# Expert tiles of 128 rows instead of 256 in a mixture-of-experts block, up and down projections alternating in halves

## The reference

```python
x = x + tanh(g_xattn) * cross_attention(layernorm(x), ctx, frac, ...)      # 16 x 128 rows of 256
xf = layernorm(x).reshape(2048, 256)
top_w, top_i = top_k(xf @ gate_w + gate_b, 2)                              # 2 of 8 experts per row
combine = sum(softmax(top_w)[:, :, None] * one_hot(top_i, 8), axis=1)
for e in range(8):
    h = gelu(xf @ w1[e] + b1[e])                                           # 256 -> 1024
    out = out + combine[:, e:e + 1] * (h @ w2[e] + b2[e])                  # 1024 -> 256
shared = gelu(xf @ ws1 + bs1) @ ws2 + bs2
x = x + tanh(g_ffn) * (out + shared)
```

## Time and profile before

| | us |
|---|---|
| device time, median of 3 runs | 719.77 |
| lowest and highest of them | 719.32, 729.58 |
| span of the profiled execution, first to last instruction | 702.4 |
| median less the span (the profiled execution has no other time recorded) | 17.4 |

### The profile page before, as it was taken

How to read it: one execution, slowest core, us unless ns; L and a number is a source line. 1 busy time by engine, 2 the same in 40 slices (tenths; PEclk the granted TensorE clock), 3 DMA queues, 4 the chain that set the end, 5 groups by cost and what they waited for, 6 DMA issues and landing times.

```text
span 702.4 us, 16222 instructions
## 1 busy us (share of the span) xinstructions
PE 652.4 (93%) x4755; PEld 557.8 (79%) x4767; DVE 449.9 (64%) x1444; ACT 348.5 (50%) x1026; POOL 327.7 (47%) x291
## 2 busy tenths in 40 slices
PE   4799999999999999996969999999999999999991
PEld 3698888998888888895545656999898998989880
DVE  2987535468789588547796854866575665655640
ACT  2567554376678577534853756433243342433410
POOL 4596525357676666513677743233232332323323
PEclk9679555599899698556898999999999999999996
DMA  8022221022233223101234458332332323323222
GB/s 270 32 66 65 65 64 52 11 65 64 64 89 101 54 72 85 46 31 45 79 125 158 142 174 215 121 61 33 58 46 44 60 35 54 55 34 45 24 24 30
DMA packets 44514, 51.91 MB, mean 74 GB/s; under 512 B 9281, under 2 KB 38593, under 8 KB 44353
## 3 DMA queue, kind: packets, MB, share of 16 engines
q1 hardware_dynamic: 36320, 41.23, 20.9%
q0 software_dynamic: 8160, 10.26, 8.6%
HBM read 32.79 MB, written 18.69 MB: 73 GB/s over the span
## 4 chain that ended last, share of the span: by engine, by line
PE 76%; DVE 10%; issue 4%; ACT 3%; POOL 2%; DMA 1%; SPq 0%; DVEq 0%; ACTq 0%; POOLq 0%
PE bank L1113 69%; PE bank L1173 5%; DVE W L805 3%; ACT W L611 1%; PE bank L1326 1%; DVE hbuf L903 1%; DVE W L775 1%; DMA out<-xres 1%; PE bank L1193 1%; DMA out<-xres,idu 1%; POOL out L547 1%; ACT W L590 0%; DVE xT L910 0%; PE bank L1254 0%; SPq L346 0%
## 5 line engine op out<-in xcount | busy, mean ns | idle before, releaser
L1113 PE MATMUL bank<-W 128*128 128x16 f32 (+3 forms) x1408 | 258.4, 335 | 13.7 <-DMA W<-wproj 9.0
L1113 PEld LDWEIGHTS bank<-W 128*128 128x128 f32 (+1 forms) x1408 | 228.0, 238 | 47.2 <-issue 21.6
L547 POOL DMA_INDIRECT out<-xres,idu x46 | 75.0, 1631 | 176.9 <-issue 152.8
L716 ACT ACTIVATE hbuf<-bank,b1t 128x256 f32<-128x256 f32 x184 | 77.3, 471 | 151.8 <-PE bank L1113 142.0
L1113 PE MATMUL bank<-xres,W 128*128 128x256 bf16 x1104 | 124.3, 273 | 1.4 <-DVE xres L1057 1.4
L1113 PE MATMUL bank<-W,xT 128*128 x1104 | 124.1, 273 | 0.0
L611 ACT ACTIVATE W<-W,mn 128x128 f32<-128x128 f32 x256 | 99.6, 396 | 45.9 <-DVE mn L805 45.9
L1113 PEld LDWEIGHTS bank<-xres,W 128*128 x1104 | 107.9, 98 | 14.2 <-issue 1.7
L1113 PEld LDWEIGHTS bank<-W,xT 128*128 128x128 bf16 x1104 | 108.0, 98 | 12.3
L805 DVE CUSTOM_DVE_ANT_0 W<-W 128x128 f32<-128x128 f32 x192 | 80.8, 473 | 5.5 <-DVE W L775 2.6
L775 DVE SCALAR_TENSOR_TENSOR W<-W,and_,bank 128x128 f32<-128x128 f32 x192 | 53.7, 340 | 44.7 <-PE bank L1113 44.7
(11 more groups left out here) (121 smaller groups left out, 679.6 us busy)
## 6 DMA issues: line engine op xcount, KB each, us to landing
stage<-wts SPq DMA_DIRECT2D x36, 512.0 KB
xres<-xs_dram SPq DMA_DIRECT2D x23, 256.0 KB, 3.3
xs_dram<-hbuf SPq DMA_DIRECT2D x14, 387.0 KB, 5.3
xres<-x SPq DMA_DIRECT2D x4, 512.0 KB, 7.0
W<-ctxT SPq DMA_DIRECT2D x16, 128.0 KB, 4.4
out<-xres SPq DMA_DIRECT2D x4, 512.0 KB, 5.1
W<-frac SPq DMA_DIRECT2D x16, 64.0 KB, 4.7
W<-wproj SPq DMA_DIRECT2D x4, 256.0 KB, 6.5
```

The source lines that it names most:

```text
L547: nc.gpsimd.indirect_dma_start(out, bass.IndirectOffsetOnAxis(idu[:, par, t:t + 1], axis=0), ysb[par][t], None, compute_op=ALU.add).then_i ...
L716: ins = nc.scalar.activation(hbuf[:, q % 2, c * TR:(c + 1) * TR], bank[q][:, c * TR:(c + 1) * TR], ACT.Gelu, bias=b1t[:, par, 2 * q + c:2 ...
L1113: return nc.tensor.matmul(o, a, b, start=start, stop=stop, **kw)
```

## The change

`TR` becomes 128: 39 tiles of 128 rows (32 + 7) in place of 23 of 256. A tile's up projection moves 128 columns with each matmul instead of 256, so a PSUM bank holds four chunks, and a tile needs two banks (`UPS = 2` parts of `UC = 4` chunks); even tiles use banks 0 and 1, odd tiles banks 2 and 3, and `up_part(j)` waits for the gelu of tile j-2 where `up_tile(j)` waited for that of tile j-1. On TensorE `body(j)` now does the first half of up of tile j, the transposes of tile j+2, the first half of down of tile j-1, the second half of up of tile j, the second half of down of tile j-1. Both `base_of` reads stand at the start of the body. Each tile has one block of 128 rows, so GpSimd starts one indirect transfer per tile. The core of the diff:

```diff
-TR = 256
+TR = 128
 TH = TR // P
+UPS = 2
+UC = HC // UPS
...
-                for q in range(4):
-                    act.wait_ge(up_ps, 4 * j + q + 1)
-                    if not (first(j) and q < 2):
-                        act.wait_ge(h_ready, 4 * j + q - 1)
-                    for c in range(2):
-                        ins = nc.scalar.activation(hbuf[:, q % 2, c * TR:(c + 1) * TR], bank[q][:, c * TR:(c + 1) * TR],
-                                                   ACT.Gelu, bias=b1t[:, par, 2 * q + c:2 * q + c + 1])
+                for q in range(UPS):
+                    act.wait_ge(up_ps, UPS * j + q + 1)
+                    if not first(j):
+                        act.wait_ge(h_ready, UPS * (j - 1) + q + 1)
+                    for c in range(UC):
+                        ins = nc.scalar.activation(hbuf[:, q, c * TR:(c + 1) * TR], bank[UPS * par + q][:, c * TR:(c + 1) * TR],
+                                                   ACT.Gelu, bias=b1t[:, par, UC * q + c:UC * q + c + 1])
...
-            def up_tile(j, par):
-                base = base_of(j)
-                pe.wait_ge(xs_lo, j + 1)
-                for q in range(4):
+            def up_part(j, par, base, q):
+                if q == 0:
+                    pe.wait_ge(xs_lo, j + 1)
+                if not first(j, 2):
+                    pe.wait_ge(g_ready, UPS * (j - 2) + q + 1)
+                elif par == 1:
+                    pe.wait_ge(acc_half, GROUPS - 1)
+                for h in range(UC):
+                    n = 0
+                    for wpart, xpart in ((0, 0), (0, 1), (1, 0)):
+                        for c in range(DC):
+                            ins = mm(bank[UPS * par + q][:, h * TR:(h + 1) * TR], w_up(base, wpart, c, UC * q + h),
+                                     xsT[par][:, (xpart * DC + c) * TR:(xpart * DC + c + 1) * TR], n == 0, n == 5)
+                            n += 1
+                ins.then_inc(up_ps, 1)
+
+            def down_part(j, par, base, q):
+                if q == 0:
+                    if not first(j, 2):
+                        pe.wait_ge(y_ready, j - 1)
+                    else:
+                        pe.wait_ge(acc_half, GROUPS)
+                pe.wait_ge(h_ready, UPS * j + q + 1)
+                for c in range(UC * q, UC * (q + 1)):
+                    for hpart, wpart in ((0, 0), (1, 0), (0, 1)):
+                        at = (hpart * HC + c) * TR
+                        ins = mm(bank[4 + par][:, 0:D], hs[par][:, at:at + P], w_down(base, wpart, c),
+                                 c == 0 and hpart == 0 and wpart == 0, c == HC - 1 and wpart == 1, skip_group_check=True)
+                if q == UPS - 1:
+                    ins.then_inc(down_ps, 1)
+
+            def body(j, par, more):
+                up_base = base_of(j)
+                if not first(j):
+                    down_base = base_of(j - 1)
+                for q in range(UPS):
+                    up_part(j, par, up_base, q)
+                    if q == 0 and more == 2:
+                        turn_tile(j + 2, par)
                     if not first(j):
...
-            def body(j, par, more):
-                up_tile(j, par)
-                if more == 2:
-                    turn_tile(j + 2, par)
-                if not first(j):
-                    down_tile(j - 1, 1 - par)
+                        down_part(j - 1, 1 - par, down_base, q)
```

More of the change, by code:

```diff
@@ L361, in _ @@
                     load_piece(i, k)
-                    write_pads((i - 1) * PAD_TILES, PAD_TILES, (k,))
+                    if k < TH:
+                        write_pads((i - 1) * PAD_TILES, PAD_TILES, (k,))
             write_pads((PAIRS - 1) * PAD_TILES, TILES - (PAIRS - 1) * PAD_TILES)
@@ L1081, in weigh @@
                 both = xres[:, GD + TH * par * D:GD + TH * (par + 1) * D].rearrange("p (t d) -> p t d", d=D)
-                nc.vector.tensor_tensor(both, bank[4 + par][:].rearrange("p (t d) -> p t d", d=D),
+                nc.vector.tensor_tensor(both, bank[4 + par][:, 0:TH * D].rearrange("p (t d) -> p t d", d=D),
                                         b2f[:, bass.ds(e * D, D)].rearrange("p (o d) -> p o d", o=1).to_broadcast([P, TH, D]),
@@ L1351, in base_of @@
                 return (e + 1) * WS
-            def up_tile(j, par):
-                base = base_of(j)
-                pe.wait_ge(xs_lo, j + 1)
-                for q in range(4):
-                    if not first(j):
-                        pe.wait_ge(g_ready, 4 * (j - 1) + q + 1)
-                    elif q == 2:
-                        pe.wait_ge(acc_half, GROUPS - 1)
-                    for h in range(2):
-                        n = 0
-                        for wpart, xpart in ((0, 0), (0, 1), (1, 0)):
-                            for c in range(DC):
-                                ins = mm(bank[q][:, h * TR:(h + 1) * TR], w_up(base, wpart, c, 2 * q + h),
-                                         xsT[par][:, (xpart * DC + c) * TR:(xpart * DC + c + 1) * TR], n == 0, n == 5)
-                                n += 1
-                    ins.then_inc(up_ps, 1)
@@ L1370, in down_tile @@
-            def down_tile(j, par):
-                base = base_of(j)
-                if not first(j, 2):
-                    pe.wait_ge(y_ready, j - 1)
-                else:
-                    pe.wait_ge(acc_half, GROUPS)
-                y = [bank[4 + par][:, t * D:(t + 1) * D] for t in range(TH)]
-                for c in range(HC):
-                    if c % 2 == 0:
-                        pe.wait_ge(h_ready, 4 * j + c // 2 + 1)
-                    for hpart, wpart in ((0, 0), (1, 0), (0, 1)):
-                        for t in range(TH):
-                            at = (hpart * HC + c) * TR + t * P
-                            ins = mm(y[t], hs[par][:, at:at + P], w_down(base, wpart, c),
-                                     c == 0 and hpart == 0 and wpart == 0 and t == 0, c == HC - 1 and wpart == 1, skip_group_check=True)
-                ins.then_inc(down_ps, 1)
@@ L1400, in _ @@
             tiles(pe, body)
-            down_tile(TILES - 1, (TILES - 1) % 2)
+            last_base = base_of(TILES - 1)
+            for q in range(UPS):
+                down_part(TILES - 1, (TILES - 1) % 2, last_base, q)
 def kernel(**inputs):
```

18 lines of the change are left out of this document (9 added, 9 removed).

## The result

| device time, us | median | lowest to highest | executions |
|---|---|---|---|
| before | 720.11 | 718.01 to 729.58 | 6 |
| changed | 773.23 | 765.55 to 806.07 | 6 |

The ratio of the changed kernel's time to the time before is 1.0668, 95% interval 1.0565 to 1.077. The forecast of a slowdown holds; the predicted 788.6 us is 15 us too high, and the measured median lies 2 us under the range that was given. The profiled execution of the changed kernel is one of its two long ones (800.88 us of device time, span 798.9), the ratio leaves those out, and the two traces are therefore compared stage by stage.

What follows compares the result with a forecast made beforehand. TensorE's array bounded the kernel before; its sequencer would pace the changed routed experts. The terms 71.7 - 0.6 - 2.3 = +68.8 us on a 702.4 us span give 771, with 17.4 added 788.6 us; range 775 to 815.

Steps and rivals of the forecast that it cites:

- What bounds the stage: Routed experts: TensorE's array before, 10.92 us a tile; after, its sequencer, with register steps 129 ns apart; chance 80%.
- Rival 1: Routed experts: array sets the pace, steps some 70 ns apart, stage 214 us, kernel 681 us; 5%.
- Part 1: Routed experts' matmuls: 128 columns take 55 ns, array 5.5 us a tile, but nothing gained under the sequencer.
- Part 2: Routed experts: TensorE's sequencer work doesn't halve, 8.3 us a tile; stage 322 us against 250.4, +71.7 us.
- Rival 3: Routed experts: TensorE's clock drops to 1.2 GHz, 10.7 us a tile; held throughout, kernel 884 us; 8%.
- Part 3: Routed experts: interleaving up and down in halves, and the banks, only moves waits; costed at nothing.
- Part 4: GpSimd's transfers in the routed experts: 39 instead of 46, 4.6 us a tile, hidden under 8.3.
- Part 5: Start and end of the routed experts: first copy and subtraction -0.6 us, last transfers -2.3 us.
- the term for all that lies outside the stage: Everything but the routed experts: carried over unchanged through the 702.4 us span and the 17.4 us added to it.
- the 17.4 us between span and median: Whole kernel: distance from the profiled 702.4 us span to the median device time, added unchanged to the forecast.

Runs made afterwards that it cites:

- experiment 2: Changed kernel with constant weight addresses on TensorE, no expert-number reads or register steps: routed experts' stage 217.2 us for 328.7, device median 672.3 us.
- experiment 4: Changed kernel with four weight addresses computed in one register instruction, serving six matmuls: routed experts' stage 229.9 us, device median 693.71 against 720.81 before.
- fixed_expert_128: The kernel of experiment 2: changed kernel with every tile using the first expert's weights at constant addresses; stage 217.2 us, device median 672.3 us.
- extra_reads_256: Kernel before with six more reads of the expert's number per tile on TensorE's sequencer: stage 316 us, device time 791.8 us.
- whole_parts_128: Changed kernel without alternating halves (all of up, transposes, all of down): stage 325.3 us against 329.1, device time 792.8 us.
- experiment 6: Alternating in halves removed, from the changed kernel (stage 325.3 us against 329.1) and from its variant with few register steps (223.4 against 229.9).
- experiment 7: Changed kernel with few register steps and its two reads apart: stage 221.6 us, median 703.72; kernel before with few steps: stage 250.2 us.
- experiment 1: Both kernels run again unedited: routed experts' stage 250.3 us before and 329.1 changed; device medians 723.4 and 794.3 us.

## Why the prediction was right, and where it was wrong

**What bounds the stage: right.** The step's pace read from the kernel before (129 ns with an empty queue and beside a running array) came back as about 127 in the changed kernel, and the removal of all register work took off 111 us (experiment 2), the thinning of the steps alone 99 (experiment 4). Rival 1 fell with that. Its sum "from 105 ns a step and down nothing is lost" doesn't follow from the terms of a tile: 6.4 us less the 2.1 for reads and waits, over 48 steps, is about 90 ns.

**Part 1, 55 ns for a matmul of 128 columns: right,** 56 measured over a stream, and 5.5 us a tile for the array alone (217.2 / 39 = 5.57 with the ends). As the part said, none of it was gained while the sequencer set the pace.

**Part 2, +71.7 us for the stage: right in kind, 6.6 short** (78.3). The timeline of TensorE before the first stretch of low clock has the starts of three tiles:

```profile
504.46 2.18 PE L1116 MATMUL bank<-xres,W 128*128 128x128 bf16 x24 [1.60 <-DVE xres L1060]
...
512.69 2.16 PE L1116 MATMUL bank<-xres,W 128*128 128x128 bf16 x24 [1.03 <-issue]
...
521.29 2.50 PE L1116 MATMUL bank<-xres,W 128*128 128x128 bf16 x24 [1.66 <-DVE xres L1060]
```

The tile without the loop's branch at its end takes 8.23 us, close to the 8.3 of the prediction; the one with it takes 8.60. The branch is the term that was put at nothing: the 0.9 us for the way to the next tile were read from the earlier trace rows, where none stands in between (483.8 to 484.9, 1.1 us). The kernel before has the other kind of seam too:

```profile
L1113 PEldq FUSED_REGOPS  x2: 46/53/60, 472.9 to 474.5; - x2
```

It takes 1.6 us. The mean of 8.42 us a tile is 38 x 0.12 = 4.4 us more than was summed. The other part is the clock: a pair of tiles with 3.4 us at 1.2 GHz takes 17.05 us, one without 16.83, and 14 such pairs make 3.1 us. The last tiles, behind the loop, take a little less (8.1 in the chain above).

Rival 3 thus came true in a small part: the clock fell, and each time the array, busy without a break at half clock (3.41 of 3.41 us), held the sequencer up. The Trainium skill, "TensorE: Matmul & The Clock Gate", section "Why this matters for your kernels", warns that a matmul stream with pauses in it falls back to the lower level. The traces agree only in part. The clock did fall with 1.0 to 1.7 us of idle array at each tile's start, and stayed at 1.00 in the kernel before and in fixed_expert_128 without such gaps; but it also stayed at 1.00 in extra_reads_256, which had gaps of 0.8 to 1.7 us twice a tile, and read 0.97 in whole_parts_128. What decides is open.

**Part 3, halves at nothing: right,** or worse than nothing by 3.8 to 6.5 us (experiment 6). **Part 4, GpSimd hidden: right,** even at 5.5 us a tile, where 4.6 were reckoned to lie just under it (experiment 7). **Part 5: -2.9 us predicted,** 2.3 of it at the end, where 1.1 were measured; the 0.6 at the start lie in the shared expert's stretch, which differs by more than that between executions (94 to 104 us), so no run shows them.

**The step that failed is the term for all that lies outside the stage, which was carried over as fixed and had nothing in the range.** In the sum it is "on a span of 702.4 us" plus "the 17.4 us between span and median": 702.4 - 250.4 + 17.4 = 469.4 us, less Part 5. The range took in the stage's uncertainty alone (9 us for a quicker step below, 10 to 25 above). Less the stage of the traces (250.4 and 328.7 us), the medians leave 469.7 us before and 444.5 after, 25 us less. In the group of experiment 1 the same difference leaves 470.5 and 465.2 us. The stage was 6.6 us longer than predicted and not shorter, so the miss at the lower end (773.23 under 775) comes from the outside term, and the two errors in part cancel: with the measured stage and end the same sum would have been 797 us.

What the 17.4 us are was misread as well, though this does the sum no harm, since 719.77 + 68.8 is the same 788.6. They were put down to start and end of the execution, which are about 2 us in every run. The rest was the distance between one execution with a short attention part (335 us) and the others: the same program has shown spans of 702.4 and 726.2 us with a stage that agrees to 0.1 us, and device times from 689 to 744 us over all its runs. A range with this spread in it would have held 773.23. Counted from the profiled execution alone the sum would have been 704.4 + 68.8 = 773.2 us, which agrees by luck: the short execution that it starts from and the stage that was summed too low together made up for the short executions after.

Why the time outside the stage was so short in the first group after the change is not settled. If the rest was as in the profile, attention took some 326 to 336 us in the four quickest executions (spans of 763.6 to 773.7 us); only their totals are known. The kernel before had such executions too (by the same reckoning some 320 us in the one of 689.0 us). That the change itself shortens the earlier stages is borne out by no trace: attention shows no difference by tile size (experiment 1), and the shared expert took 95.6 to 104.1 us with 256 rows and 94.4 to 102.1 with 128.

## What to carry to other kernels

Halving a tile halves the array's work but not the addresses: before shrinking a matmul whose operand is addressed through a register, count the register instructions, the reads and the loop's branch per tile, and multiply by their spacing (not their duration) where the queue is empty. Compare each long pause with the sequencer's lead, and not only their sum with the array's time. If the sequencer is the bound, put several addresses into one fused register instruction ahead of the matmuls, and keep two reads and a branch from standing behind one another. And set a forecast against the stage of the change, with the spread of all the other stages in its range.

## What the runs showed of the hardware that I had not expected

- A register instruction on TensorE's sequencer costs some 127 ns with its matmuls when it shows 46 ns, and at most 13 ns less (by the stage) when it shows 32; four addresses in one instruction show 55 ns and serve six matmuls. The number of instructions is what counts.
- The sequencer's lead over the array was about 2 us with matmuls of 256 columns: a pause of 3.0 us idled the array for 0.79 us ahead of an up part, one of 3.3 us for 1.68 ahead of a down part, and with pauses of 2.1 us ahead of every other down part a stage of 23 tiles lost 7.4 us.
- The branch of a loop shows 215 ns on TensorE's sequencer, and the way from one tile's last step to the next one's first takes 2.3 us with it and 1.7 without.
- TensorE's clock fell to 1.2 GHz for 3.4 us in every 17 us, with great regularity, for 14 times in the stage of the changed kernel, and stayed at 2.4 GHz in a stage with gaps of 0.8 to 1.7 us twice a tile (extra_reads_256). Gaps alone don't foretell it.
- Attention, which no edit touched, took from 333 to 368 us over the profiled executions, with a mean clock that explains it only in part: 335 us at 0.76, 365 at 0.70, but 342 at 0.91.
- The named releaser of a gap can be a bystander: 1.66 us "from DVE xres L1060" were the sequencer's own branch and two reads, and fell away with the register work.
